# First mixture of a two-layer decoder: where the logits, half of the split rows and the sigmoid's table are made

## The reference, cut to what matters

```python
x = x + _L0_xattn_ref(_layernorm(x), ctx_768, ...)      # 16 heads of 8, softmax over 77 keys
x = x + _L0_ffn_ref(_layernorm(x), ...)

# _L0_ffn_ref, 16 experts, 8 chosen per token, inner width 128, and one shared expert
gates = jnp.einsum('bsd,ed->bse', x, gate_w)            # the logits
scores = jax.nn.sigmoid(gates)
_, inds = jax.lax.top_k(scores + expert_bias, 8)
selected = scores at inds, divided by their sum, times 2.826
combine = selected spread back over the 16 experts, zero elsewhere
h = silu(x @ w_gate[e]) * (x @ w_up[e]);  y = sum over e of combine[e] * (h @ w_down[e])
y = y + silu(x @ shared_gate_w) * (x @ shared_up_w) @ shared_down_w
```

## Time and profile before

| | |
|---|---|
| median of 3 runs | 562.66 us (561.68 to 565.26) |
| profiled execution, its own time | 561.79 us |
| its span | 560.0 us, 9954 instructions |
| TensorE matmul busy | 474.9 us, 85% |
| VectorE busy | 371.4 us, 66% |
| ScalarE busy | 332.6 us, 59% |
| GpSimd busy | 266.6 us, 48% |
| mean granted TensorE clock | 0.916 of full |

### The profile page before, as it was taken

How to read it: one execution, slowest core, us unless ns; L and a number is a source line. 1 busy time by engine, 2 the same in 40 slices (tenths; PEclk the granted TensorE clock), 3 DMA queues, 4 the chain that set the end, 5 groups by cost and what they waited for, 6 DMA issues and landing times. The chain is left out here.

```text
span 560.0 us, 9954 instructions
## 1 busy us (share of the span) xinstructions
PE 474.9 (85%) x3161; PEld 359.5 (64%) x3161; DVE 371.4 (66%) x910; ACT 332.6 (59%) x655; POOL 266.6 (48%) x294
## 2 busy tenths in 40 slices
PE   4589999999578866899995999675588779999995
PEld 2577888876356645588883578453466556677774
DVE  4787777774746743566666377757467454999995
ACT  3687777775437754355552465214377555998983
POOL 1699879777434651366562660113063320745410
PEclk9799999999759995999996899796899959999999
DMA  6614342424265000344422200002580002111101
GB/s 186 202 47 120 99 119 76 124 82 129 73 140 144 1 2 1 118 137 134 124 94 64 60 2 0 1 1 72 135 226 2 2 2 71 27 54 38 38 0 37
DMA packets 34688, 41.80 MB, mean 75 GB/s; under 512 B 5178, under 2 KB 26612, under 8 KB 34420
## 3 DMA queue, kind: packets, MB, share of 16 engines
q1 hardware_dynamic: 33796, 40.65, 25.9%
q10 hardware_dynamic: 848, 0.60, 0.4%
HBM read 30.70 MB, written 8.18 MB: 69 GB/s over the span
## 5 line engine op out<-in xcount | busy, mean ns | idle before, releaser
L1276 POOL TENSOR_TENSOR e_gc<-e_g,e_c 128x512 f32<-128x512 f32 x32 | 42.1, 1316 | 41.9 <-ACT e_g L1259 22.4
L2063 DVE TENSOR_TENSOR e_h_lo<-e_h,e_h_hi 128x512 fp32r<-128x512 f32 x56 | 55.9, 1050 | 3.6 <-ACT e_h_hi L1941 3.6
L1756 POOL TENSOR_TENSOR m_w_hi<-m_w,m_one 128x512 fp32r<-128x512 f32 x16 | 19.2, 1201 | 69.6 <-DMA m_w<-in_L_ffn_W 49.6
L963 ACT ACTIVATE x_pT<-x_turn 77x1024 f32<-77x1024 f32 x32 | 32.7, 1021 | 32.1 <-PE x_turn L901 32.1
L1937 ACT ACTIVATE e_h<-e_h,m_b 128x512 f32<-128x512 f32 x64 | 43.8, 690 | 9.3 <-PE e_h L1837 9.2
L557 ACT ACTIVATE a_p<-xn_all,a_least 128x128 f32<-128x128 f32 x128 | 40.9, 392 | 6.5 <-DVE a_least L596 6.4
L901 PE MATMUL x_turn<-consts,x_p 128*77 128x128 f32 x256 | 38.8, 299 | 3.9 <-ACT x_p L968 3.9
L1235 ACT ACTIVATE e_h_hi<-e_h 128x512 fp32r<-128x512 f32 x34 | 21.5, 634 | 33.7 <-DVE e_h L1318 28.1
L1324 DVE TENSOR_TENSOR e_h_lo<-e_h,e_h_hi 128x512 fp32r<-128x512 f32 x34 | 23.8, 699 | 26.1 <-ACT e_h_hi L1235 26.1
L703 POOL TENSOR_TENSOR a_p<-a_p,a_r 128x512 f32<-128x512 f32 x32 | 33.3, 1041 | 15.1 <-DVE a_r L605 15.1
L901 PEld LDWEIGHTS x_turn<-consts,x_p 128*77 128x77 f32 x256 | 30.8, 160 | 13.3 <-ACT x_p L968 12.5
(11 more groups left out here) (299 smaller groups left out, 1444.3 us busy)
## 6 DMA issues: line engine op xcount, KB each, us to landing
e_c<-spread SPq DMA_DIRECT2D x32, 256.0 KB, 3.2
x_ks<-kstack SPq DMA_DIRECT2D x16, 462.0 KB, 5.6
kstack<-a_blk_hi SPq DMA_DIRECT2D x32, 154.0 KB, 3.0
m_w<-in_L_ffn_W SPq DMA_DIRECT2D x16, 256.0 KB, 3.0
a_raw<-in_experts SPq DMA_DIRECT2D x17, 192.0 KB, 2.4
kstack<-a_blk_lo SPq DMA_DIRECT2D x16, 154.0 KB, 2.9
su_reversed<-scratch SPq DMA_DIRECT2D x1, 1024.0 KB, 5.8
w_wkv<-in_L_attn_Wkv SPq DMA_DIRECT2D x1, 1024.0 KB, 8.0
```

What stands on the lines that cost most here:

```text
L963: act.activation(pT[k % 2][:, :, :], tb[0:NKV, :, :], ACT.Copy).then_inc(S["turned_out"], 1)
L1276: pool.tensor_tensor(gc[k % 2][:, :], g[u % 2][:, :], c[k % NC][:, :], ALU.mult).then_inc(S["weighted"], 1)
L2063: dve.tensor_tensor(h_lo[half][f][:, :], h[half][f], h_hi[half][f][:, :].bitcast(F32), ALU.subtract).then_inc(S["lo_done"], 1)
```

## The change

`mixture0` now makes a helper object with the methods that `cross_attention` calls, and itself calls the cross attention of layer 0 with it. The logits of each batch are computed in the drain into the cross attention's turn bank and copied to SBUF (`raw_logits`); the high parts of both halves and the low part of half 0 are made there too; a new hook, `table`, is called by ScalarE behind its step 19 and loads the sigmoid's table. In layer 1 the new hook does nothing. In the mixture TensorE begins with the wait for the split weights and unit 0, ScalarE takes the sigmoid from `raw_logits`, VectorE makes the low part of half 1, and the turn of the weights of half 0 no longer waits for the sigmoid.

```diff
--- before.py
+++ after.py
@@ -967,6 +967,8 @@
                             act.wait_ge(S["turn_done"], since["turn_done"] + n - 1)
                         act.activation(p[n % 2][:, :, :, :], s[n % 2][:, :, :, :], ACT.Exp,
                                        scale=SC).then_inc(S["exp_done"], 1)
+                    if ahead is not None and n == STEPS + 3:
+                        ahead.table(act)
 
             @block.vector
             def _(dve):
@@ -1088,8 +1090,8 @@
             ctx0 = (sb0("ctxT", [CKV + 1, B * NKV]), sb0("wv", [CKV + 1, 2 * P]))
             setup_sems = setup_and_bias(bias0, w0, ctx0)
             past_sems = attention0(bias0, w0, ctx0, setup_sems)
-        cross_attention(0, past_sems=past_sems)
-        mixture0(nc, tools, spread0, x_all, xnT_all, consts, tables, we_hi, we_lo, we_split)
+        mixture0(nc, tools, spread0, x_all, xnT_all, consts, tables, we_hi, we_lo, we_split,
+                 lambda ahead: cross_attention(0, past_sems=past_sems, ahead=ahead))
         attention1(nc, a, tools, layer_norm, x_all, xn_all, xnT_all, consts, rows, cols, eps_pow, pick)
         mixture1(nc, a, tools, cross_attention, x_all, xn_all, xnT_all, consts, tables)
         store()
@@ -1111,7 +1113,7 @@
             left = rest[:, :, 0:experts]
 
 
-def mixture0(nc, tools, spread, x_all, xnT_all, consts, tables, w_hi, w_lo, w_split):
+def mixture0(nc, tools, spread, x_all, xnT_all, consts, tables, w_hi, w_lo, w_split, cross_attention):
 
     ident = consts[:, 0:P]
     _, _, _, _, gate_w, ebias, _, _, _, routing = tables
@@ -1127,6 +1129,41 @@
     with ExitStack() as st:
         sb, ps, sem = tools(st, "e0_")
         x_hi, x_lo = (sb(n, [P, T], F32R) for n in ("x_hi", "x_lo"))
+        raw_logits = sb("raw_logits", [P, B, E0])
+        logits_out = sem("logits_out")
+
+        class Ahead:
+
+
+            def splits(self, pool):
+                pass
+
+            def table(self, act):
+                act.preload_act_table(ACT.Sigmoid)
+
+            def logits(self, pe, b, bank):
+                mm = pe.matmul(bank[:, 0, E0 * b:E0 * b + E0], xnT_all[:, P * b:P * b + P], gate_w[:, :], start=True,
+                               stop=True)
+                if b == B - 1:
+                    mm.then_inc(routing["logits_done"], 1)
+
+            def logits_out(self, dve, bank):
+                dve.wait_ge(routing["logits_done"], 1)
+                dve.tensor_copy(raw_logits[:, :, :], bank[:, 0, 0:B * E0].rearrange("p (b e) -> p b e", b=B)).then_inc(
+                    logits_out, 1)
+
+            def high_half(self, act, half):
+                part = slice(HALF * half, HALF * half + HALF)
+                act.activation(x_hi[:, part], xnT_all[:, part], ACT.Copy).then_inc(routing["x_hi_done"], 1)
+
+            def low_half(self, dve, half):
+                part = slice(HALF * half, HALF * half + HALF)
+                dve.wait_ge(routing["x_hi_done"], half + 1)
+                dve.tensor_tensor(x_lo[:, part], xnT_all[:, part], x_hi[:, part].bitcast(F32),
+                                  ALU.subtract).then_inc(routing["x_lo_done"], 1)
+
+        ahead = Ahead()
+        cross_attention(ahead)
         scores, sel, left, mask, comb = (sb(n, [P, B, E0]) for n in ("scores", "sel", "left", "mask", "comb"))
         best = sb("best", [P, B, 8])
         total = sb("total", [P, B])
@@ -1140,7 +1177,6 @@
         ub = [ps(f"up{j}") for j in range(3)]
         yb = [ps(f"y{j}") for j in range(2)]
         rb = ps("route")
-        logits = rb[:, 0:B * E0].rearrange("p (b e) -> p b e", b=B)
         names = ("scored", "step", "combined", "spread_out", "gate_done", "up_done", "gated", "weighted", "made",
                  "hi_done", "lo_done", "y_done", "yT_out", "turn_done", "added") + tuple(f"c_landed{j}" for j in range(NC))
         S = {n: sem(n) for n in names} | routing
@@ -1192,9 +1228,7 @@
 
             def combine_turned(half):
                 pe.wait_ge(S["combined"], half + 1)
-                if half == 0:
-                    pe.wait_ge(S["scored"], 1)
-                else:
+                if half == 1:
                     pe.wait_ge(S["wT_ready"], 1)
                 for b in range(HB):
                     mm = pe.transpose(rb[0:E0, P * b:P * b + P], comb[:, HB * half + b, :], ident)
@@ -1209,9 +1243,6 @@
                     mm = pe.transpose(rb[:, P * b:P * b + P], yT[half][:, P * b:P * b + P], ident)
                 mm.then_inc(S["turn_done"], 1)
 
-            for b in range(B):
-                mm = pe.matmul(logits[:, b, :], xnT_all[:, P * b:P * b + P], gate_w[:, :], start=True, stop=True)
-            mm.then_inc(S["logits_done"], 1)
             pe.wait_ge(w_split, 2 * (E0 + 1))
             for u in range(N + LAG):
                 if u < N:
@@ -1243,11 +1274,8 @@
                 act.wait_ge(S["y_done"], LAST_OF[half] + 1)
                 act.activation(yT[half][:, :], yb[half][:, :], ACT.Copy).then_inc(S["yT_out"], 1)
 
-            act.wait_ge(S["logits_done"], 1)
-            act.activation(scores[:, :, :], logits, ACT.Sigmoid).then_inc(S["scored"], 1)
-            for half in range(2):
-                part = slice(HALF * half, HALF * half + HALF)
-                act.activation(x_hi[:, part], xnT_all[:, part], ACT.Copy).then_inc(S["x_hi_done"], 1)
+            act.wait_ge(logits_out, 1)
+            act.activation(scores[:, :, :], raw_logits[:, :, :], ACT.Sigmoid).then_inc(S["scored"], 1)
             act.preload_act_table(ACT.Silu)
             for u in range(N + 1):
                 if u < N:
@@ -1277,11 +1305,7 @@
 
         @block.vector
         def _(dve):
-            for half in range(2):
-                part = slice(HALF * half, HALF * half + HALF)
-                dve.wait_ge(S["x_hi_done"], half + 1)
-                dve.tensor_tensor(x_lo[:, part], xnT_all[:, part], x_hi[:, part].bitcast(F32),
-                                  ALU.subtract).then_inc(S["x_lo_done"], 1)
+            ahead.low_half(dve, 1)
             steps = [0]
 
             def own_values(*made):
```

## The result

The changed kernel took 560.11 us (median of 13 runs, 558.21 to 563.60), the kernel before 562.66 (13 runs, 560.54 to 565.26). The ratio is 0.9949 with a 95% interval of 0.9930 to 0.9968, so 1.8 to 3.9 us less, 2.9 in the middle. A second measurement in a later batch gave 0.9957 (0.9930 to 0.9983). Forecast were 560.6 us and 2.1 us less. The profiled execution took 559.68 us, its span is 557.9 us, of 9954 instructions as before.

What follows compares the result with a forecast made beforehand. The prediction took a serial stretch of 5.27 us between join and first gate as what counts, not engine shares. -5.27 + 3.50 - 0.3 = -2.1 us from the 562.66 us median gave 560.6 us, own range 559.7 to 561.8.

Steps and rivals of the forecast that it cites:

- The head: Between join and first gate of layer 0's mixture: logits, first halves and sigmoid wait leave, -5.27 us.
- The drain and the join: Layer 0's cross attention end: moved work delays the mixture's start as in layer 1, 1.12 + 1.15 + 1.23 = 3.50 us.
- The clock term: TensorE's granted clock in layer 0's drain: a fall nearer to layer 1's returns 0.3 us of up to 0.8.
- the 211.6 to 211.9 of the forecast: Sign in layer 0's drain: the residual add of batch 7 starts at 211.6 to 211.9 for 209.60.
- The slack of the routing: Mixture's start: half 0's routing weights are ready 3.5 us before TensorE turns them.
- The prediction's estimate from that page: Drain's table load: at about 2.66 us per switch ScalarE is free at 209.7, ahead of 210.1, the sum unchanged.
- The anchor: Mixture's start: TensorE's order holds the 32 routed halves 6.55 us behind the first gate, so all move with it.
- rival 2: Behind the gate: VectorE's queue and half 1's routing 0.65 us later, gain 1.1 us, or a later anchor, near 0; chance 0.13.
- Behind the gate, 0: After the first gate: low half 1 ahead of the routing, sigmoid and Silu's load there were costed at nothing.
- The sum: Whole change: -5.27 + 3.50 - 0.3 = -2.1 us, bounds -0.9 and -3.0.
- rival 1: Layer 0's drain keeps its pace, only the join's 1.23 us is paid: gain 4.0 us, 558.6 us; chance 0.12.

Runs made afterwards that it cites:

- e2_end: Changed kernel with all eight logits of layer 0 at step 24, behind everything else of the drain; ratio to the kernel before 0.995.
- e5_turn_early: Changed kernel with the routing weights of half 0 turned behind unit 1's products instead of unit 2's; ratio to the kernel before 0.9963.
- e7_warm: Changed kernel with 16 unread products of 512 columns in idle places of TensorE's drain in layer 0; ratio to the kernel before 0.9963.
- e10_early_late: Changed kernel with half 0's routing weights turned behind unit 1 and half 1's behind unit 4; ratio to the kernel before 0.9927.
- e9_turn_late: Changed kernel with only half 1's routing weights turned one unit later, behind unit 4's products; ratio to the kernel before 0.9957.
- e3_no_table: Changed kernel without the hook's table load in the drain, so the sigmoid's table loads behind the join; ratio to the kernel before 0.9978.
- e1_holes: Changed kernel with layer 0's logits behind the output products, where TensorE stands idle in the drain; ratio to the kernel before 0.9965.
- e6_holes_both: Changed kernel with the logits behind the output products in the drains of both layers; ratio to the kernel before 0.991.
- e4_splits_in_head: Changed kernel with both high and both low halves back behind the join, only logits and table load in the drain; ratio to the kernel before 0.9989.
- e11_best: Changed kernel with logits behind the output products in both layers and both turns of routing weights moved; 555.52 us, ratio to the kernel before 0.985.

## Why the prediction was right, step by step

**The head, -5.27 us.** Right: nothing of it is left, and the second profile of before has it unchanged. The gate load is the mixture's first TensorE instruction, 1.43 us behind the last evacuation's end, for 1.50 by layer 1.

**The drain and the join, +3.50, with the clock +3.2.** Right within the scatter. The mixture's start moved from 7.89 and 8.44 us behind E (first logits load) to 11.60 and 11.41: +3.3 by the means. The output product of batch 6 starts 2.55 us behind E for 1.44, 1.11 later, and layer 1 has it at 2.55 too. That this place in the queue is the cause was only read off layer 1 in the prediction; the two runs that move the logits show it, and the run with the splits in the head shows that the splits have no part in it.

**The clock term, -0.3.** The first pair of profiles has it with the other sign: the add is 2.56 us late, not 2.0, since the clock fell 2.6 us behind E. In the second profile of before it also fell at 2.6, and the differences there are 1.8 to 2.0. What I took for a property of layer 0 was one draw: thirteen of the fourteen profiles have this fall 2.2 to 2.9 us behind E, and the one at 5.0 was the one I read. That the add came at 211.59, at the edge of the 211.6 to 211.9 of the forecast, is luck: this execution entered the drain 0.57 us sooner. Counted from E, it would stand at 212.16 in the time of the profile before, outside that range. The prediction also counts layer 1's rise as 6.0 us in one place and 5.8 in another: 6.0 is from the block's first small load at 453.65, 5.8 from its first dense product, 0.2 us later.

**The slack of the routing.** Right, with 3.1 us: without the table load in the drain, a routing 1.0 us later moved nothing over 0.2. In the drain the load ends at 207.65 and ScalarE then stands idle for 2.2 us until batch 7's evacuation, as forecast. At the head the load runs from 216.68 to 217.96, right behind the sigmoid's end at 216.67, and silu starts at 218.18 after 0.21 us that it owes to the gate product. Layer 1's mixture has a load with ScalarE's work close on both sides (in the kernel before):

```profile
454.46 1.28 ACT L1953 ACT_TABLE_LOAD   x1
455.76 0.69 ACT L1937 ACTIVATE e_h<-e_h,m_b 128x512 f32<-128x512 f32 x1
```

The instruction ahead of it ends 0.02 us before, the one behind starts 0.01 us after. So a switch costs 1.28 us here. The Trainium skill ("ScalarE: Activation LUTs", "What ACT_TABLE_LOAD costs") counts some 1.4 us of drain beside the load. These rows leave no room for it on either side. (The prediction's estimate from that page should read 209.6 and not 209.7, by its own terms; nothing hangs on it.)

**The anchor.** This is the step that failed in its mechanism, though the time came out. I had written that the pipeline is anchored 6.55 us behind the first gate by the turn of half 0's weights. What moved rigidly with the first gate is the next stage: 83.8 us behind it in both profiles of the changed kernel and in the five variants that leave the order of the turns alone and keep the table load in the drain (both runs with the holes, all logits at the end, the split head, the fillers: 83.74 to 83.84). But the turn is not what holds it: 1.3 us sooner, or 2.1 with the fillers, changed nothing. What holds it are two waits that end at nearly the same place, TensorE's for the routing of half 1 and the one for the product behind the first broadcast: moving both turns, and only both, brought the next stage to 82.08. The fall of the clock in the first wait is not a third: the kernel before waits 1.93 and 1.92 us there, its clock does not fall, and unit 6's gate product still starts 17.4 and 17.8 us behind the gate load, for 17.6 and 17.5 in the changed kernel. I had the wait in rival 2 and priced only its lateness by the low half.

**Behind the gate, 0.** In fact -0.98 us by the means. All but 0.1 of it lies at the mixture's end: from the last unit's gate product to the next stage 10.09 and 9.95 us before, 9.11 and 9.12 changed. The last down product and the turn of the outputs in the kernel before:

```profile
298.99 0.62 PE L1173 MATMUL e_y<-e_h_hi,we_hi 128*128 128x512 f32 x1 [1.03 <-DVE e_h_lo L1324]
...
301.16 1.11 PE L1209 MATMUL e_route<-consts,e_yT 128*128 128x128 f32 x4 [0.69 <-ACT e_yT L1244]
```

and in the changed one:

```profile
296.96 0.50 PE L1209 MATMUL e_y<-e_h_hi,we_hi 128*128 128x512 f32 x1 [1.03 <-DVE e_h_lo L1348]
...
298.61 0.65 PE L1243 MATMUL e_route<-consts,e_yT 128*128 128x128 f32 x4 [0.69 <-ACT e_yT L1275]
```

The granted clock fell at 299.2 in the kernel before, inside the last down product, so the turn of the outputs took 1.11 us; in the changed kernel it fell at 299.7, when that turn (0.65 us) was over. The other traces bear this out, though no run was made for it. The sooner the clock falls ahead of the next stage, the longer this end is, in all fourteen profiles:

| the clock falls, ahead of the next stage | profiles | last unit's gate product to next stage |
|---|---|---|
| 1.0 us or less, or behind its start | changed (both), `e2_end`, `e5_turn_early`, `e7_warm`, `e10_early_late` | 9.11 to 9.12 us |
| 1.4 to 2.0 us | `e9_turn_late`, `e3_no_table`, `e1_holes`, `e6_holes_both`, `e4_splits_in_head` | 9.22 to 9.52 us, in this order |
| 3.1 us | `e11_best` | 9.61 us |
| 3.8 and 4.1 us | before (both) | 9.95 and 10.09 us |

So this part of the gain is the place of the clock's fall, not work taken away. Why the clock falls sooner in the kernel before (80.6 and 81.1 us behind the gate load, 83.2 and 83.6 in the changed kernel) no run shows.

**The sum.** -1.93 ahead of the gate for a forecast of -2.1, and -0.98 that I did not have. The interval of the measured 2.9 us (1.8 to 3.9) holds both the forecast and the sum of the two, so the total alone could not have told that the second part exists. That rival 1 (the drain keeps its pace) would not come was decided by layer 1's rows, and the holes show what it needs: not idle time, but a place in the queue behind the product that the chain waits for.

## What to carry to other kernels

If the same helper already runs elsewhere in the program, align the two places on a common event and subtract; that priced the part of this change ahead of the gate to a few tenths of a microsecond. Moving work into a drain where the engine has idle time is not enough: here it was free only behind the instruction that the chain waits for, and ahead of it the same work cost 1.9 us. And a lone saving at the start of a pipeline was worth nothing here while a second wait ended at the same place; try the two moves together before dropping either.

## What the runs showed beyond that

**Untouched stages differ by up to 6 us between profiles.** From the first attention operation of layer 1 to its last 128x512 evacuation, fourteen profiles took 139.0 to 145.3 us with the same instructions throughout (in two runs layer 1's logits stand elsewhere, behind this stretch). The first 75 us of it (length, busy, granted clock, DMA share, GB/s), in the kernel before and in the run with the late turn alone:

```profile
303.30:378.30 75.00, 60.63 (x340) 0.89 0.09 24
```

```profile
300.30:375.30 75.00, 63.43 (x340) 0.85 0.09 24
```

A mean clock of 0.89 or 0.85 goes with 75.7 or 78.3 us for the attention stage. Its length is not spread evenly: it took 75.4 to 76.0 us in seven profiles (0.89) and 77.8 to 79.5 us in the other seven (0.84 to 0.86), and nothing lies between. The rest lies in the cross attention (63.3 to 67.0 us to its E), where TensorE waits 4.3 to 7.0 us in all for loads of keys, 4.3 in the first profile of the kernel before and 7.0 in that of the late turn. A profile's total can't judge a change of 2 us here; the stretches between fixed events can.

**GpSimd beside VectorE.** The same 128x1 power on GpSimd, with the low half running on VectorE and without, in the changed kernel:

```profile
209.57 0.68 DVE L1162 TENSOR_TENSOR e_x_lo<-xnT_all,e_x_hi 128x512 fp32r<-128x512 f32 x1
...
209.74 0.94 POOL L1068 TENSOR_TENSOR rstd<-var,eps_pow 128x1 f32<-128x1 f32 x1 [3.01 <-DVE var L1035]
...
212.70 0.56 POOL L1068 TENSOR_TENSOR rstd<-var,eps_pow 128x1 f32<-128x1 f32 x1 [1.12 <-DVE var L1035]
```

0.94 us for 0.56. It is so in all fourteen profiles: the 25 powers that overlap a low half took 0.93 or 0.94 us, the other 199 took 0.56 to 0.58. It lay off the chain.
